# 32-head attention: the turned probabilities as the stationary operand

## The reference

```
q = apply_axial_rope((x @ Wq).reshape(b, n, 32, 8), pos_map)
k = apply_axial_rope(k.reshape(b, n, 32, 8), ctx_pos_map)     # k, v = split(ctx @ Wkv)
logits = einsum('bqhd,bkhd->bhqk', q, k) / sqrt(8)
w = softmax(logits, axis=-1)
attn = einsum('bhqk,bkhd->bqhd', w, v).reshape(b, n, 256)
return attn @ Wout + bout
```

## Time and profile before

| | before |
|---|---|
| median of 3 runs | 2931.08 us (2929.55 to 2933.55) |
| profiled execution, its own time (first to last instruction = span) | 2940.2 us |
| TensorE busy, loads | 82%, 50% |
| VectorE, ScalarE, GpSimd busy | 45%, 41%, 38% |
| 32-head attention, first to last maximum (L973) | 563.0 to 946.0 us |

### The profile page before, as it was taken

The page is one execution under the profiler, slowest core; times in us unless marked ns, Lnnn a source line. Parts: engine busy times, 40 slices in busy tenths (PEclk is TensorE's granted clock), DMA queues, the critical chain, the costliest instruction groups (busy, mean ns, idle before and its releaser), DMA issues.

```text
span 2940.2 us, 35906 instructions
## 1 busy us (share of the span) xinstructions
PE 2404.5 (82%) x10553; PEld 1482.8 (50%) x10596; DVE 1328.7 (45%) x3445; ACT 1212.1 (41%) x4398; POOL 1106.2 (38%) x1087
## 2 busy tenths in 40 slices
PE   5999999788898899989999997899948765723653
PEld 4666668544443344456666664466634323302542
DVE  2443442577777333434444433433366755730112
ACT  3444442466666112255555552233326552601111
POOL 3211110244444000133335352245524555446665
PEclk8999999999999999999999998999969866756887
DMA  9910000100000200000000003356541000003766
GB/s 347 350 52 1 1 1 1 40 1 1 1 1 1 106 1 1 0 1 1 1 1 31 1 31 97 114 100 104 95 126 62 8 8 1 8 8 71 152 142 145
DMA packets 159442, 162.76 MB, mean 55 GB/s; under 512 B 26931, under 2 KB 151107, under 8 KB 158484
## 3 DMA queue, kind: packets, MB, share of 16 engines
q1 hardware_dynamic: 127124, 119.64, 13.6%
q0 software_dynamic: 32128, 40.82, 7.7%
HBM read 81.35 MB, written 79.10 MB: 55 GB/s over the span
## 4 chain that ended last, share of the span: by engine, by line
issue 34%; PE 16%; DVE 7%; DMA 4%; POOL 4%; ACT 3%; another core or an unknown queue 1%; SPq 1%; POOLq 0%; DVEq 0%; ACTq 0%
PE ps L133 12%; DMA moe_sum<-work,weights 3%; ACT work L948 2%; POOL slots L2631 2%; POOL work L2708 1%; DMA work<-xn_rows,weights 1%; PE ps L883 1%; PE ps L2069 1%; POOL moe_sum L2722 1%; PE ps L2084 1%; DVE n_mx L973 1%; DVE xn L249 1%; DVE weights L2679 0%; DVE weights L998 0%
## 5 line engine op out<-in xcount | busy, mean ns | idle before, releaser
L133 PE MATMUL ps<-work,weights 128*128 128x512 f32 (+5 forms) x2176 | 817.5, 541 | 20.7 <-ACT work L948 11.4
L133 PE MATMUL ps<-xn_T,weights 128*128 128x512 f32 (+5 forms) x1392 | 576.4, 554 | 27.6 <-DMA weights<-in_L_ffn_Wd 7.2
L133 PEld LDWEIGHTS ps<-work,weights 128*128 128x128 f32 (+3 forms) x2188 | 328.8, 195 | 260.0 <-issue 200.7
L948 ACT ACTIVATE work<-ps,n_negm 128x128 f32<-128x128 f32 (+2 forms) x1024 | 334.4, 362 | 213.5 <-DVE n_negm L976 213.1
L133 PE MATMUL ps<-weights,work 88*128 (+4 forms) x1472 | 397.2, 395 | 4.8 <-DVE weights L430 3.3
L133 PEld LDWEIGHTS ps<-xn_T,weights 128*128 128x128 f32 (+3 forms) x1392 | 254.5, 195 | 212.4 <-issue 182.1
L1030 POOL TENSOR_TENSOR work<-work,n_rinv 128x512 f32<-128x512 f32 (+2 forms) x256 | 216.0, 856 | 295.0 <-DVE n_rinv L982 294.0
L714 POOL TENSOR_TENSOR work<-work,rinv 128x512 f32<-128x512 f32 x128 | 133.5, 1043 | 310.4 <-DVE rinv L665 284.0
L133 PEld LDWEIGHTS ps<-weights,work 128*128 128x128 f32 (+2 forms) x1472 | 228.0, 196 | 39.1 <-issue 7.2
L948 ACT ACTIVATION_READ_ACCUMULATOR work<-ps,n_negm 128x1 f32 x1024 | 226.3, 227 | 0.0
L255 POOL TENSOR_TENSOR rstd<-var,neg_half 128x4 f32<-128x4 f32 x32 | 35.3, 1102 | 424.7 <-DVE var L240 424.7
(11 more groups left out here) (297 smaller groups left out, 3620.0 us busy)
## 6 DMA issues: line engine op xcount, KB each, us to landing
f_rows<-weights SPq DMA_DIRECT2D x17, 2176.0 KB, 19.3
weights<-in_L_ffn_gate_up_proj SPq DMA_DIRECT2D x16, 768.0 KB
work<-f_rows SPq DMA_DIRECT2D x80, 136.0 KB
weights<-in_L_ffn_W SPq DMA_DIRECT2D x96, 88.0 KB
weights<-in_L_ffn_down_proj SPq DMA_DIRECT2D x16, 384.0 KB
f_sum<-weights SPq DMA_DIRECT2D x2, 2176.0 KB, 15.2
moe_sum<-weights POOLq DMA_DIRECT2D x2, 2176.0 KB
weights<-in_L_xattn_Wo SPq DMA_DIRECT2D x2, 2048.0 KB, 12.4
```

Of the source, the lines that this page charges most:

```text
L133: return nc.tensor.matmul(out, lhsT, rhs, start=start, stop=stop, skip_group_check=True)
L948: last = nc.scalar.activation(n_p[:, i, j, lo:hi], S_BANKS[t % 3][:, j * P + lo:j * P + hi], ACT.Exp, bias=n_negm[:, i, m:m + 1], scale=sc ...
```

## The change

For the 32-head attention a class `Slim` and its lists take the place of `Narrow`. The turned probabilities of a head (128 keys x 128 queries) become the stationary operand, and its 8 value columns with a column of ones beside them the moving one, so that column 9 of each output is the sum. The score products are issued one per step, before the turns of the unit three steps back; values follow four steps late. Once per batch VectorE takes the reciprocals of the 32 sums and multiplies the outputs; TensorE turns them (two turns), ScalarE copies them, and the output product follows. Gone are the sums in the exponentials, the reciprocals per unit, the division on GpSimd, the head mask and the sum over heads, and the padded values. `tail_t` becomes 10, the output product comes at step 7. `n_rinv` is renamed where `Narrow` still uses it.

```diff
+    P_LAG = 3
+    PV_LAG = 4
+    NORM_LAG = 5
+    O_LAG = 6
+    OUT_AT = O_LAG + 1
+    def slim_out(blk):
+        return (B7, Y[1])[blk % 2]
+    def slim_pe(pe, S, q_t, v_one, o_t, beside):
...
+        for t in S.steps:
+            if S.new:
...
+                done(pe, A.p_ready, s, before)
+                mm(S_BANKS[t % 3], q_t[r0:r0 + A.rows, hf, b * P:(b + 1) * P],
+                   n_kblk[r0:r0 + A.rows, c % 2, :, :].rearrange("p h k -> p (h k)")).then_inc(A.s_mm.sem, 1)
+            u = t - P_LAG
+            if S.has(u):
+                done(pe, A.p_ready, s, u)
+                done(pe, A.pt_ready, s, u - 1)
+                for j in range(NB):
+                    last = nc.tensor.transpose(B6[:, j * P:(j + 1) * P], n_p[:, u % 4, j, :], ident[:])
+                last.then_inc(A.pt_tr.sem, 1)
+            u = t - PV_LAG
+            if S.has(u):
+                blk, g = u // A.groups, u % A.groups
+                done(pe, A.pt_ready, s, u)
...
+                for j in range(NB):
+                    h = g * NB + j
+                    last = mm(slim_out(blk)[:, h * A.vw:(h + 1) * A.vw], n_pt[:, u % 2, j * P:(j + 1) * P], v_one[:, blk % TB, h, :])
+                last.then_inc(A.o_mm.sem, 1)
+            u = t - O_LAG
+            blk = A.last_of(u)
+            if S.has(u) and blk is not None:
+                done(pe, A.on_ready, s, blk)
+                for hf in range(KD):
+                    last = nc.tensor.transpose(slim_out(blk)[:, hf * P:(hf + 1) * P], n_on[:, blk % 2, hf * P:(hf + 1) * P], ident[:])
+                last.then_inc(A.o_tr.sem, 1)
...
+    def slim_act(act, S, scale, o_t, beside):
...
+        def turned(u):
+            blk = A.last_of(u)
+            if S.has(u) and blk is not None:
+                done(act, A.o_tr, s, blk)
...
+                nc.scalar.activation(o_t[:, :, b * P:(b + 1) * P], slim_out(blk)[:, 0:D].rearrange("p (k c) -> p k c", k=KD), ACT.Copy)\
+                    .then_inc(A.ot_ready.sem, 1)
+        for t in S.steps:
...
+            turned(t - O_LAG - 1)
...                          # copy of the turned bank, even units
+            if S.new:
...
+                for j in range(NB):
+                    last = nc.scalar.activation(n_p[:, i, j, :], S_BANKS[t % 3][:, j * P:(j + 1) * P], ACT.Exp,
+                                                bias=n_negm[:, i, j:j + 1], scale=scale)
+                last.then_inc(A.p_ready.sem, 1)
+    def slim_dve(dve, S, scale, beside):
...
+            u = t - NORM_LAG
+            blk = A.last_of(u)
+            if S.has(u) and blk is not None:
+                o = slim_out(blk)[:, 0:A.heads * A.vw].rearrange("p (h d) -> p h d", d=A.vw)
+                done(dve, A.o_mm, s, u)
+                link(nc.vector.reciprocal(n_rinv, o[:, :, A.hd]))
+                done(dve, A.o_tr, s, blk - 2)
+                nc.vector.tensor_tensor(n_on[:, blk % 2, :].rearrange("p (h d) -> p h d", d=A.hd), o[:, :, 0:A.hd],
+                                        n_rinv.unsqueeze(2).broadcast_to([P, A.heads, A.hd]), ALU.mult).then_inc(A.on_ready.sem, 1)
...                          # maximum, negation, copy of the turned bank, odd units
-    l1_v = tile(R1, 0, TB * KD * 4 * P).rearrange("p (t h r c) -> p t h r c", t=TB, h=KD, r=4)
+    l1_v = tile(R1, 0, TB * L1H * (L1HD + 1)).rearrange("p (t h d) -> p t h d", t=TB, h=L1H)
-    L1 = Narrow("a1", 2, L1H, P, l1_wout, l1_bias, 9)
+    L1 = Slim("a1", 2, L1H, l1_wout, l1_bias, 10)
-        for r in range(4):
-            c = slice(r * P // 4, (r + 1) * P // 4)
-            ins = nc.scalar.activation(l1_v[:, j * CB:(j + 1) * CB, :, r, c], v[:, :, :, r, :], ACT.Copy)
-        ins.then_inc(l1_v_ready.sem, 1)
+        nc.scalar.activation(l1_v[:, j * CB:(j + 1) * CB, :, 0:L1HD], TP.rearrange("p (t h d) -> p t h d", t=CB, h=L1H), ACT.Copy)\
+            .then_inc(l1_v_ready.sem, 1)
-        nc.gpsimd.memset(l1_v, 0.0).then_inc(pool_consts, 1)
+        nc.gpsimd.memset(l1_v, 1.0).then_inc(pool_consts, 1)
```

More of the change, by code:

```diff
@@ L1035, in narrow_pool, with __init__, last_of @@
             beside(S, t)
+    class Slim:
+        def __init__(self, name, stage, heads, wout, bias, tail_t):
+            self.name, self.stage, self.heads, self.wout, self.bias = name, stage, heads, wout, bias
+            self.hd = D // heads
+            self.vw = self.hd + 1
+            self.rows = NB * self.hd
+            self.per_half = P // self.rows
+            self.groups = KD * self.per_half
+            self.n, self.late = TB * self.groups, O_LAG + 1
+            self.units = TB * KD
+            self.needs_qk, self.needs_v = {}, {}
+            self.tail_t = tail_t
+            n = self.n
+            self.chain = signal("attn_chain", n + TB)
+            self.kblk_ready = signal("narrow_kblk_ready", self.units)
+            self.s_mm = signal("attn_s_mm", n)
+            self.negm_ready = signal("attn_negm_ready", n)
+            self.p_ready = signal("attn_p_ready", n)
+            self.pt_tr = signal("attn_pt_tr", n)
+            self.pt_ready = signal("attn_pt_ready", n)
+            self.o_mm = signal("attn_o_mm", n)
+            self.on_ready = signal("slim_on_ready", TB)
+            self.o_tr = signal("slim_o_tr", TB)
+            self.ot_ready = signal("narrow_ot_ready", TB)
+            self.y_mm = signal("attn_y_mm", KD)
+        def last_of(self, u):
+            return u // self.groups if u % self.groups == self.groups - 1 else None
@@ new lines, in _build, with out_product @@
+    P_LAG = 3
[3 more added lines that the diff above has]
+    OUT_AT = O_LAG + 1
+    n_on = tile(WK, 4096, 512).rearrange("p (n d) -> p n d", n=2)
+    def slim_out(blk):
+        return (B7, Y[1])[blk % 2]
+    def slim_pe(pe, S, q_t, v_one, o_t, beside):
+        A, s = S.A, S.s
+        def out_product():
+            done(pe, A.ot_ready, s, -1)
+            for k in range(KD):
+                for hf in range(KD):
+                    last = mm(Y[k], A.wout[:, hf, k * P:(k + 1) * P], o_t[:, hf, :], hf == 0, hf == KD - 1)
+                last.then_inc(A.y_mm.sem, 1)
+        for t in S.steps:
+            if S.new:
+                c, r, b, hf = place(A, t)
+                r0 = r * A.rows
+                if t in A.needs_qk:
+                    done(pe, A.needs_qk[t][0], s, A.needs_qk[t][1])
+                if r == 0:
+                    done(pe, A.kblk_ready, s, c)
+                before = t - 3 if t >= 3 else max(i for i in range(A.n - 3, A.n) if i % 3 == t) - A.n
+                done(pe, A.p_ready, s, before)
[12 more added lines that the diff above has]
+                done(pe, A.pt_ready, s, u)
+                if u in A.needs_v:
+                    done(pe, A.needs_v[u][0], s, A.needs_v[u][1])
+                if g == 0:
+                    done(pe, A.ot_ready, s, blk - 2)
+                    if blk == 1:
+                        done(pe, yt_ready, S.n, 1)
+                for j in range(NB):
[6 more added lines that the diff above has]
+                done(pe, A.on_ready, s, blk)
+                for hf in range(KD):
+                    last = nc.tensor.transpose(slim_out(blk)[:, hf * P:(hf + 1) * P], n_on[:, blk % 2, hf * P:(hf + 1) * P], ident[:])
+                last.then_inc(A.o_tr.sem, 1)
+            if S.tail and t - A.tail_t in (0, 1):
+                tail_pe_y(pe, S.n, t - A.tail_t)
+            if S.tail and t - A.tail_t in (4, 5):
+                tail_pe_xn(pe, S.n, t - A.tail_t - 4)
+            beside(S, t)
+            if S.old and t == OUT_AT:
+                out_product()
+        if not S.new:
+            out_product()
@@ new lines, in slim_act, with out_of_y @@
+    def slim_act(act, S, scale, o_t, beside):
+        A, s = S.A, S.s
+        def out_of_y(n, k):
+            done(act, yt_tr, n - 1, 1)
+            done(act, A.y_mm, s, k - KD)
+            g = A.stage // 2
+            nc.scalar.activation(YT[:, k, :], Y[k], ACT.Identity, scale=gates[:, g:g + 1], bias=A.bias[:, k:k + 1])\
+                .then_inc(yt_ready.sem, 1)
+        def turned(u):
+            blk = A.last_of(u)
+            if S.has(u) and blk is not None:
+                done(act, A.o_tr, s, blk)
+                if blk == 0:
+                    done(act, A.y_mm, s, -1)
+                b = blk % TB
+                nc.scalar.activation(o_t[:, :, b * P:(b + 1) * P], slim_out(blk)[:, 0:D].rearrange("p (k c) -> p k c", k=KD), ACT.Copy)\
+                    .then_inc(A.ot_ready.sem, 1)
+        for t in S.steps:
+            if S.old and t - OUT_AT in (1, 2):
+                out_of_y(S.n, t - OUT_AT - 1)
+            turned(t - O_LAG - 1)
+            u = t - P_LAG
+            if u % 2 == 0 and S.has(u):
+                done(act, A.pt_tr, s, u)
+                done(act, A.o_mm, s, u - 2)
+                nc.scalar.activation(n_pt[:, u % 2, :], B6, ACT.Copy).then_inc(A.pt_ready.sem, 1)
+            if S.new:
+                i = t % 4
+                done(act, A.negm_ready, s, t)
```

(58 more changed lines are left out.)

16 lines of the change are left out of this document (8 added, 8 removed).

## The result

The changed kernel takes 3183.6 us (median of 4 runs, 3178.66 to 3188.04) against 2932.3 for the kernel before: ratio 1.0847, 95% interval 1.0828 to 1.0866. It is 251 us slower. The direction was forecast, the size was not: 3045 with a range to 3150. The profiled execution has a span of 3186.3 us.

A forecast was written before the change was run, and what follows sets the result against it. No engine was full in plain steps; the chain set them at 2.2 us against 1.73 of TensorE work. Forecast stage: 370 at full clock + 112 half-clock units + 15 bursts = 497 against 383, +114, so 3045 us, range 2925 to 3150.

The forecast's parts named there:

- the latency won: Shorter chain per step of the 32-head attention: about 1.5 us less latency, worth at most 0.5 us per plain step, 60 us.
- The unit at full clock: TensorE's work per 4 heads by 128 queries after the change: turns 0.44, scores 0.86, values 0.90, together 2.20 us.
- the score product: Issued singly with nothing beside it, it was to cost a unit the full 0.86 us instead of 0.43.
- the unit of before: TensorE's work per unit in the earlier kernel: turns 0.44, values 0.86, half a score pair 0.43, together 1.73 us.
- The unit at half clock: Extra TensorE time per unit when the granted clock is halved: +1.4 to +2.3 us, taken as 1.9.
- The count of units at half clock: Units of the stage run at the lower clock: 13 per group, 20 in the last, 59 in all, 112 us.
- Open: The 14 steps per group whose clock level was left undecided; a little under half, 6, were counted as half clock.
- the bursts: Runs of wide products of other work, expected to raise the clock; those beginning at half clock were to cost 15 us.
- the stage without the fall: The 32-head attention at full clock throughout: four groups of 92.4 us, 370 us against 383 before.
- Rival B: Half clock in all but the bursts: about 104 units x 1.9 us, kernel 3131 us (3170 at 2.3 per unit); chance 0.18.
- A: Rival: the clock stays full because loads and turns keep the engine counted as busy; stage 370, kernel 2918 us; chance 0.14.
- rival C: The single score product still costs 0.43 us because a load or turns slip beside it; kernel 2880 us; chance 0.03.

The follow-up runs named there:

- experiment 9: The changed kernel with score products over all 128 rows of queries and key blocks instead of 32, values still 9 columns: 2920.3 us, ratio 0.996 to the kernel before.

## Why the prediction was wrong

- What bounds before, and that the latency won is worth nothing: right. The other engines' work fell as listed, and the step is TensorE's own work.
- The unit at full clock, 2.20: 2.44 measured. The term mis-sized is the score product, 0.86 by the spacing of the earlier trace rows; it is 1.06, since the next load is not pulled ahead of a product of 32 rows. The earlier trace rows had it: 1.13 and 1.12 us stood there, and from 561.78 the next record starts 1.06 us later. The same holds for the pair, so the unit of before is 0.1 us more than the 1.73 of the sum. Values 0.88 (0.90 forecast) and turns 0.50 (0.44) were nearly right.
- The unit at half clock: +1.9 forecast from bounds of 1.4 and 2.3, +2.11 measured (4.55 less 2.44). The loads slow down with the clock, which the bound of 2.3 had: the eight value records take 1.65 against 0.88.
- The count of units at half clock, which is the step that failed: "Open: 4, 8 to 12, 23, 24 and 26 to 31: 14, a little under half of them, 6", 59 units in all. Of the 542 us at half clock, records of units fill about 434, which is 95 units of 4.55. Had all 14 open steps been counted, the same count would have given 91. I took the level in the open steps for a coin toss. It is not: this stream does not hold the full clock by itself. Of the stretches at full clock none lasted longer than 14 us; after each burst it fell within a few steps and came back only at a later burst.
- What the excess of 133 us over the forecast (247.5 against 114) is made of, as an estimate from these figures: 95 units x 2.11 = 200 where 112 stood, +88, of which the count makes 76 and the price of a unit 12. The other 108 us at half clock are the wide products and the turns of the tail: at most half of that, some 54, where 15 stood for the bursts, +39. The rest, 630.5 - 200 - 54 = 376, is the stage without the fall, where 370 stood, +6; that it is so near is luck in part, since 0.24 us too little per unit is 31 us by itself, and other terms must have been too large.
- Rival B ("half clock in all but the bursts", chance 0.18, 3131 to 3170) had the mechanism and came closest. Its 104 units x 1.9 = 198 equals the 200 above by two errors that cancel, 9 units too many and 0.21 us too little for each; what it lacked was the bursts and the other work at half clock.
- The rows named against A were the right ones: 17 us at 0.50 with records for 80% was the stage's later state in small.
- The single score product (rival C) does not slip beside anything: right. New work per batch, filling (1.06 us for 1152 columns) and the copy of the values: cheap, as forecast; experiment 9 ends 15 us below before with all of them in it.
- That all of it passes to the end: right, the stage grew by 247.5 us and the profiled execution by 246.1.

## What to carry to other kernels

Judge a change of operands on TensorE by what it streams, not only by how long it keeps the engine: a form with more loads and few columns can leave the engine busy to 99% and at half speed. When a load is the price, try a wider moving operand and look at the granted clock; here 119 useless columns per product cost 0.1 us a unit and gave back 225 us, while with 55 and single scores the clock of the stage was 0.78. And products of 32 rows belong in pairs, since each lone one costs as much as two (1.06 us).

## What the runs showed of the hardware that I had not expected

- Work taken away made the kernel slower: 36 columns instead of 512 in one product per unit, +34 us, clock 0.94 to 0.69.
- The same instruction stream ran at either level in one execution (64 columns: 4.6 and 2.5 us per plain step): a burst brought it up, and it could fall without any wait of TensorE.
- Score products over 128 rows are cheaper than over 32 when products of 128 rows follow: 0.94 us against 1.06 (922.96 to 923.90, and 1088.47 to 1089.53).
